# Attention of layer 2: the output jobs, projections, roundings and splits of the next group at other steps

## The reference, cut to what matters

```python
h = _rms(x, ln_w)
q = (h @ wq).reshape(B, S, NHEADS, HEAD_DIM)      # 32 heads of 64
k = (h @ wk).reshape(B, S, KVHEADS, HEAD_DIM)     # 8 of 64
v = (h @ wv).reshape(B, S, KVHEADS, HEAD_DIM)
q, k = _rope(q, k)
...
scores = jnp.einsum('bqhd,bkhd->bhqk', q, k) / np.float32(np.sqrt(HEAD_DIM))
scores = jnp.where(causal[None, None], scores, jnp.float32(-1e+30))
attn = jax.nn.softmax(scores, -1)
o = jnp.einsum('bhqk,bkhd->bqhd', attn, v).reshape(B, S, NHEADS * HEAD_DIM)
x = x + o @ wo
```

## Time and profile before

| | us |
|---|---|
| median of 3 runs | 3843.64 (3839.55 to 3846.38) |
| the profiled execution's own time | 3848.8 |
| its span | 3846.9 |
| busy: PE, DVE, ACT, POOL | 3325.0, 2473.0, 1949.4, 1668.8 |

### The profile page before, as it was taken

The page is one execution under the profiler, slowest core; times in us unless marked ns, Lnnn a source line. Parts: engine busy times, 40 slices in busy tenths (PEclk is TensorE's granted clock), DMA queues, the critical chain, the costliest instruction groups (busy, mean ns, idle before and its releaser), DMA issues. The chain is left out here.

```text
span 3846.9 us, 58222 instructions
## 1 busy us (share of the span) xinstructions
PE 3325.0 (86%) x18336; PEld 2631.2 (68%) x18336; DVE 2473.0 (64%) x4854; ACT 1949.4 (51%) x3927; POOL 1668.8 (43%) x1269
## 2 busy tenths in 40 slices
PE   5798798479898989988995999788889987998979
PEld 4566586148566666667883899556666666887868
DVE  4787544955577878875446656477777876445554
ACT  3787433333476767754333322266666774334333
POOL 1666211832466667742211544176666662221111
PEclk8999799889999999999996999799999999999989
DMA  2000232323101111003320000110111102332222
GB/s 79 22 30 3 77 108 64 133 91 115 60 25 31 30 27 32 20 4 120 114 73 16 1 1 1 42 35 24 25 28 27 30 12 82 115 109 83 73 94 74
DMA packets 81189, 204.66 MB, mean 53 GB/s; under 512 B 16923, under 2 KB 20123, under 8 KB 80662
## 3 DMA queue, kind: packets, MB, share of 16 engines
q1 hardware_dynamic: 80774, 201.26, 16.8%
q10 hardware_dynamic: 144, 0.07, 0.0%
HBM read 171.39 MB, written 4.69 MB: 46 GB/s over the span
## 5 line engine op out<-in xcount | busy, mean ns | idle before, releaser
L1246 POOL TENSOR_TENSOR probs<-probs,row_inverse 128x640 f32<-128x640 f32 (+7 forms) x640 | 737.4, 1158 | 538.5 <-DVE row_inverse L1272 528.1
L548 PE MATMUL psUp<-xnT_part,weights_part 128*128 128x512 f32 x3456 | 843.3, 394 | 2.8 <-DVE hidden L689 1.8
L548 PEld LDWEIGHTS psUp<-xnT_part,weights_part 128*128 128x128 f32 x3456 | 636.4, 190 | 126.1 <-issue 2.4
L525 POOL TENSOR_TENSOR weights_part<-weights,weights_part 128x768 fp32r<-128x768 f32 x136 | 251.2, 1851 | 1029.3 <-ACT weights_part L598 1029.3
L1260 DVE TENSOR_REDUCE neg_max<-psS 128x1 f32<-128x640 f32 (+7 forms) x640 | 476.8, 745 | 149.1 <-PE psS L1151 147.9
L1287 DVE TENSOR_TENSOR probsT_part<-psT,probsT_part 128x512 fp32r<-128x512 f32 (+1 forms) x960 | 502.3, 551 | 89.9 <-ACT probsT_part L1229 78.7
L1229 ACT ACTIVATE probsT_part<-psT 128x512 fp32r<-128x512 f32 (+1 forms) x960 | 436.1, 490 | 219.9 <-PE psT L1163 216.7
L1213 ACT ACTIVATE probs<-psS,neg_max 128x640 f32<-128x640 f32 (+7 forms) x640 | 475.5, 743 | 96.9 <-DVE neg_max L1260 83.2
L1147 PE MATMUL psS<-k_part,q_parts 128*128 128x512 f32 (+1 forms) x960 | 413.5, 431 | 114.1 <-ACT probs L1213 73.9
L559 PEld LDWEIGHTS psDown<-weights_part,hidden_part 128*128 128x128 f32 x3456 | 458.2, 194 | 56.0 <-issue 23.3
L559 PE MATMUL psDown<-weights_part,hidden_part 128*128 128x256 f32 x3456 | 468.0, 286 | 31.2 <-DVE hidden_part L709 31.2
(11 more groups left out here) (310 smaller groups left out, 4771.6 us busy)
## 6 DMA issues: line engine op xcount, KB each, us to landing
gates<-gate_rows SPq DMA_DIRECT2D x136, 512.0 KB, 4.0
weights<-in_l_ffn SPq DMA_DIRECT2D x148, 384.0 KB, 4.4
qk_swapped<-qk_raw SPq DMA_DIRECT2D x384, 64.0 KB, 2.0
bc_broadcast<-bc_rows SPq DMA_DIRECT2D x32, 512.0 KB, 4.6
w_group<-in_l_wgroup SPq DMA_DIRECT2D x16, 384.0 KB, 3.2
q_whole<-q_steps SPq DMA_DIRECT2D x32, 128.0 KB
w_o_group<-in_l_wo SPq DMA_DIRECT2D x16, 256.0 KB, 3.2
rope<-in_l_rope SPq DMA_DIRECT2D x2, 1024.0 KB, 5.5
```

The source lines that it names most:

```text
L525: nc.gpsimd.tensor_tensor(w[1][:, j, :], wt[:, j, :], w[0][:, j, :].bitcast(F32), ALU.subtract).then_inc(w_split, 1)
L548: last = nc.tensor.matmul(psU[:, u % 2, g, :], wp[:, j, g * D + k * P:g * D + (k + 1) * P], xp[:, k, cols(half)], start=n == 0, stop=n == ...
L1246: self.nc.gpsimd.tensor_tensor(self.p[:, n % 4, 0:w], self.p[:, n % 4, 0:w], self.rinv[:, at:at + 1].to_broadcast([P, w]), ALU.mult).then_ ...
```

## The change

It gives `L2Hooks` other step numbers. The output jobs of the first seven tiles stand one step later, at s % 4 = 1; the projections u = 2 to 5 stand one step later too, and with them the multiply of the swapped halves and the add, which are counted from them. `ROUND_AT` and `SPLIT_AT`, which `L2Hooks` had from `Splits`, are given of its own, with the pieces from the third on one step later. The instructions are the same ones, in another order on each engine. The order of PSUM banks follows from the lists.

```diff
-    PROJECT = (1, 3, 5, 7, 10, 13)
-    OUTPUT = (4, 8, 12, 16, 20, 24, 28, 31)
+    PROJECT = (1, 3, 6, 8, 11, 14)
+    OUTPUT = (5, 9, 13, 17, 21, 25, 29, 31)
+    ROUND_AT = {6: (0,), 8: (1,), 11: (2,), 13: (3,), 16: (4,), 19: (5,)}
+    SPLIT_AT = {7: 0, 12: 2, 15: 3, 18: 4, 21: 5}
```

## The result

The changed kernel takes 3864.17 us (median of 5, 3858.84 to 3870.87), the one before 3843.64. The ratio is 1.0056, 95% interval 1.0041 to 1.0071: slower by 0.56%, 20.5 us. The two profiled executions lie only 15.4 apart (3864.17 and 3848.8): the one of before was 5.2 over its own median, the changed one on it.

The account below looks back on a forecast made before the run. PE sets the pace, with 8 to 9 us of holes a group; terms of -3.3 and new waits sum to about +1.05 us a group, +14.7 us over 14 groups, giving 3858 us, range 3830 to 3874.

Parts of the forecast that it names:

- The signs named for the profile: PE waits a group: GpSimd from 1.94 to nearly nothing, exponentials 2.9 to some 4.5, split parts 1.1 to 2.6.
- Step 23, -1.94: Transposes no longer wait for GpSimd's scaling, which goes ahead of the last split; minus 1.94 us a group, bounds 0.9 to 1.94.
- Step 12, -1.16: Scores no longer wait for an exponential behind the fifth projection's raw copy; minus 1.16 us a group.
- Step 4 and 5: Bank wait at step 4 goes, minus 0.2 us; at step 5 the exponential behind project 1's copy is late, plus 0.15.
- Step 8, +0.9: Scores wait for the exponential behind the third projection, now right behind tile 1's last product; plus 0.9 us, bounds 0 and 1.16.
- the values +0.7: At step 8 the first product of tile 2 waits for VectorE to empty a bank; plus 0.7 us, bounds 0 and 1.1.
- Steps 12, 13 and 16, +0.9 and +0.4: VectorE and an exponential late at 12 and 13, plus 0.9 us; last projection's copy delays step 16's exponential, plus 0.4.
- Step 21, +1.3: Scores wait for an exponential behind the last rounding, moved to ScalarE's step 19; plus 1.3 us, bounds 0 and 1.5.
- The outputs, "I cost at nothing": Outputs at 25 and 29 and the swap transfers cost nothing; any wait that opens is 0.1 to 0.2 us.
- The faster rival: The wait at step 8 lets VectorE and ScalarE catch up, later ones don't open; -0.95 us a group, 3830; chance 0.20.
- The slower one: Late exponential at step 21 holds step 23's scaling, half of the 1.94 comes back; +2.0 us a group, 3872; chance 0.12.
- The rule weighed beside the rows: Two-SBUF-input VectorE multiplies contend with GpSimd; the one moved to step 10 would cost 0.69, not 0.95; 0.95 kept, sum otherwise 3854.5.

Follow-up runs that it names:

- e1: The kernel before, with only the split of the last piece moved from GpSimd's step 20 to 21; 3816.08 us, ratio 0.9929.
- e10: The changed kernel with the split of the last piece back at GpSimd's step 20; 3878.91 us, ratio 1.0088 to the kernel before.
- e5: The kernel before, with only the outputs of tiles 1, 3, 4, 5 and 6 one step later; 3838.0 us, ratio 0.9978.
- e2: The kernel before, with the fifth projection moved from step 10 to 11 and the split of piece 3 from 14 to 15; 3843.45 us, ratio 0.9989.
- e4: The kernel before, with only the third projection moved from step 5 to 6, the fourth staying at 7; 3857.16 us, ratio 1.0026.
- e8: The changed kernel with the last projection at step 15, not 14, and piece 4's split at 17, not 18; 3865.39 us, ratio 1.0047 to the kernel before.
- e7: The changed kernel with the third projection at step 7 instead of 6; 3843.98 us, ratio 0.9997 to the kernel before.
- e3: The changed kernel with the rounding of the last piece back at ScalarE's step 18; 3855.6 us, ratio 1.0028 to the kernel before.
- e13: The kernel before with outputs at 9, 17, 21, 25, 29, third and fourth projections at 6 and 8, piece 2's split at 12; 3879.09 us, ratio 1.0081.
- e9: The kernel before with outputs at 9, 17, 21, 25, 29 and the split of the last piece at 21; 3820.39 us, ratio 0.9939.

## Why the prediction was right, point by point

Forecast 3858, slower with 0.6; measured 3864.2, slower. The direction and most of the chains were right. On the profiled execution the sum was 3863.5 and it came to 3864.17; a group +1.05, measured +1.03. That agreement is luck: the profiled execution of before had more time at the lower clock than the changed one. Between the medians the difference is 20.5 us against 14.7 forecast, 1.46 a group, and at the full clock it is 1.54. By stretch, at the full clock:

| steps | forecast | measured |
|---|---|---|
| 4 to 11 | +0.39 | +0.41 |
| 12 to 15 | +1.3 | +1.96 |
| 16 to 19 | 0 | -0.32 |
| 20 to 23 | -0.64 | -0.36 |
| 24 to 27 | 0 | +0.24 |
| 28 to 31 | 0 | -0.41 |

The misses are 1.9 us without their signs, and with them they leave 0.5. The signs named for the profile were half right too: the waits for exponentials came to 4.1 a group (4.5 forecast), those for split parts before `values` only to 1.5 (2.6 forecast). A part of what VectorE's lateness costs shows as waits for banks, and the one in step 13 is too short to be listed.

- *Step 23, -1.94:* the wait went. e1 shows it by itself, at -1.55 for the whole group at the full clock, since 0.4 came back at step 24; in the changed kernel e10 makes the move worth 1.1, so here it was over-sized. The bound of 0.9 named for it was the better size. The +0.24 at steps 24 to 27 comes with this move: e1 has it, e5 has not.
- *Step 12, -1.16:* it went too; alone (e2) 3 us by the medians, or 8 by the groups, were left of its 16.
- *Step 4 and 5:* the waits at step 4, 0.2, are gone as said; of the +0.15 only 0.05 is listed at step 5.
- *Step 8, +0.9:* 0.88. The place and chain were right; e4 showed a condition that the prediction used but didn't name, the empty step 7. For the values +0.7 was too much, 0.28 is listed. The sum for steps 4 to 11 fits because what was too much here was too little elsewhere: the multiply of step 5 takes 1.65 us on the mean where it took 0.92, and no term had that.
- *Steps 12, 13 and 16, +0.9 and +0.4:* +1.96 in the table. This is the term most under-sized. The waits are of the kinds named, but the working took every duration as it stood, and the swapped half's multiply of step 13 takes 1.73 us on the mean, where the multiply of the same piece took 1.18 before. And "no wait for either shows ... and if one opens it is the 0.1 to 0.2" missed the projection of step 14, which waits 0.43 for the bank of the output of step 13. The 1.96 less the 0.31 that steps 16 to 19 gain by the means is 1.65. With the last projection at 15 and the multiply still long (e8) 0.7 of it stays. With the projection at 13 and the multiply long (e2) steps 12 to 19 cost 0.86. With the multiply of step 13 short and the projection still at 14 (e7) steps 13 to 15 lose 1.15 of their excess. So the long multiply and the projection of step 14 have each about a half; each of these runs moved something else as well, and the exact shares stay open.
- *Step 21, +1.3:* 1.15. e3 takes it away and gets only half back.
- *The outputs, "I cost at nothing":* this step of the argument failed. Alone they are worth -0.49 at the full clock (e5), nearly all of it at 28 to 31, by my reading through the order of banks; that it is this was not tried by itself. In the changed kernel the same 0.41 is there. The argument asked only which wait for `kept` goes, not what the output's place does to the ring of three banks.

The faster rival (lateness is paid once) falls with e13 and with the table: the wait at step 12 stays whole in e13, and in the changed kernel steps 12 to 15 are 1.96 us longer. The slower one (GpSimd's wait doesn't go) falls for the changed kernel, though e3 shows GpSimd next in line.

**The rule weighed beside the rows.** The prediction took 0.95 us for the multiply moved to step 10, the mean of four that the trace of before shows at 0.68 to 1.18. That one had taken 0.68 before, and takes 0.68 in the changed kernel, so there was nothing to gain on it. The third projection's, now at step 8, took 1.06 and takes 0.68, the first keys at step 10 took 0.87 and take 0.68; the one of step 5 went from 0.92 to 1.65, the fifth projection's, now at step 13, from 1.18 to 1.73. And step 10 is no safe place: in e7 GpSimd's add runs there and the multiply takes 1.76. All this agrees with what the Trainium skill ("SBUF — State Buffer", SBUF: two separate sides) says: whichever of a VectorE instruction with two inputs in SBUF and a GpSimd instruction that reads SBUF starts first holds the shared port pair, and the other blocks. The prediction weighed the rule at the one step where it hoped to gain, 0.27; at step 13, where the change loses 0.55, and at step 5, where it loses 0.7, it didn't look.

## What to carry to other kernels

In a hand-written pipeline a wait closed is worth what it measures only if nothing next in line is late within it: e1 kept 1.55 of 1.94, e2 0.2 (by the medians) to 0.6 (by the groups) of 1.16, and e9 got next to nothing from a second move. Before a job is put directly behind a tile's last product, look what else PE has until the chain on ScalarE is through; one projection in step 7 hid a wait of 0.9. When work moves, list for each VectorE instruction with two inputs in SBUF what GpSimd runs beside it at the new place. Compare stretches at the same granted clock: the means of 14 groups made e5's gain 1.2 us where it is 0.5, and the change's loss 1.03 where it is 1.54. And where several moves go together, take them apart: one of the change's moves alone made the kernel 0.7% faster, while all together made it 0.56% slower.

## What the runs showed of the hardware

- A listed wait on PE is shorter than the wait. Three transposes take 0.49 us and one is recorded at 0.27, so they start 0.11 apart and each record overlaps the next by 0.16. A wait between two is listed 0.16 short and below 0.31 not at all. With more and shorter waits the changed kernel hides more of them: in the sixth group, at the full clock, PE's busy time rose from 75.5 to 76.8 us for the same work.
- VectorE's multiply with two inputs in SBUF took 0.68 us where it met nothing. Where it started while GpSimd was in an instruction it ended 0.55 us after that instruction, whether 0.24 us of it were left (e7, step 13: 0.79 in all), 0.62 (before: 1.17) or 1.17 (changed: 1.72). It costs the rest of GpSimd's instruction and most of its own time. GpSimd is held too: in e7 the second instruction of the split, begun at 1276.35 while the multiply ran to 1276.82, took 1.61 us and not 1.28.
- TensorE's granted clock was at one of two levels, and in the 14 groups it fell behind a wait of PE or within one: in the kernel before, at steps 31 and 0 (a wait of 1.3 us for `oT` and in some groups one of 2.9 behind it) and at 23 and 24 (the wait of 1.9 for GpSimd). In the runs where that wait is 1.6 or less, or gone, no group has the lower level at steps 24 to 27; where it is 1.9 or more (before, e2, e4, e13), 6 to 10 of the 14 have it. In the 66 executions of the kernel before that the series list, the three with the lowest mean clock, 0.942, took 3851.9 to 3855.7 us, and the five with the highest, 0.948 and 0.949, 3837.0 to 3841.9.
